# A three-part decoder layer on one core: the first values go to psA, weights' lower halves are made a step later, the last attention step is reordered, and one shared unit moves behind the experts

## The reference

```python
x = x + attn(layernorm(x), Wq, Wk, Wv, Wr)          # 16 heads of 64, causal penalty -50, scale 1/8
x = x + xattn(layernorm(x), ctx, w_q, w_k, w_v, w_o) # the same with keys and values from ctx
x = x + ffn(layernorm(x), ...)
# ffn: shared = swiglu(z @ w_in.T) @ w_out.T         (hidden 512)
#      h = swiglu(z @ w1.T); a gate picks one of 2 groups, then the top 2 of its 4 experts
#      routed = sum over the two of h * weight @ w2[expert].T
```

## Time and profile before

| | us |
|---|---|
| median of 3 runs | 793.65 (792.72 to 795.74) |
| profiled execution | 793.49 |
| its span | 791.7 |
| PE busy in it | 757.6 |
| ACT, DVE, POOL busy | 447.2, 417.9, 281.7 |

### The profile page before, as it was taken

How to read it: one execution, slowest core, us unless ns; L and a number is a source line. 1 busy time by engine, 2 the same in 40 slices (tenths; PEclk the granted TensorE clock), 3 DMA queues, 4 the chain that set the end, 5 groups by cost and what they waited for, 6 DMA issues and landing times. The chain is left out here.

```text
span 791.7 us, 17891 instructions
## 1 busy us (share of the span) xinstructions
PE 757.6 (96%) x6371; PEld 644.6 (81%) x6371; DVE 417.9 (53%) x1265; ACT 447.2 (56%) x1475; POOL 281.7 (36%) x302
## 2 busy tenths in 40 slices
PE   6899999999999999999999999999899998999993
PEld 5688888888888788888888888888667888999883
DVE  6456465456546646543544554465668545333175
ACT  4766556566656767675566566566544435444120
POOL 1553234233422545552243244234102770000475
PEclk9999999999999999999999999999999999999997
DMA  6896000000000202000000002000050555765244
GB/s 197 319 418 225 2 0 0 0 0 0 0 0 2 80 1 81 2 29 1 1 0 26 0 0 104 2 5 24 2 213 26 196 196 184 199 200 174 79 133 140
DMA packets 33608, 64.55 MB, mean 82 GB/s; under 512 B 3412, under 2 KB 15060, under 8 KB 32980
## 3 DMA queue, kind: packets, MB, share of 16 engines
q1 hardware_dynamic: 29172, 51.01, 19.2%
q0 software_dynamic: 4096, 12.59, 4.8%
q10 hardware_dynamic: 288, 0.26, 0.1%
HBM read 38.02 MB, written 30.02 MB: 86 GB/s over the span
## 5 line engine op out<-in xcount | busy, mean ns | idle before, releaser
L445 POOL TENSOR_TENSOR prob<-prob,rsum 128x512 f32<-128x512 f32 x128 | 132.8, 1040 | 332.1 <-DVE rsum L664 332.1
L541 ACT ACTIVATE prob<-psS,nmin 128x128 f32<-128x128 f32 x512 | 182.3, 385 | 21.3 <-DVE nmin L642 15.2
L625 DVE TENSOR_TENSOR oT_lo<-psW,oT_hi 128x512 fp32r<-128x512 f32 x64 | 44.2, 690 | 156.4 <-ACT oT_hi L527 156.3
L541 ACT ACTIVATION_READ_ACCUMULATOR prob<-psS,nmin 128x1 f32 x512 | 115.3, 225 | 0.0
L519 ACT ACTIVATE v<-psW 128x512 f32<-128x512 f32 x64 | 38.2, 597 | 83.4 <-PE psW L144 83.4
L793 PE MATMUL psS<-kt,q 64*128 64x128 f32 x1024 | 74.4, 285 | 0.9 <-DVE kt L617 0.9
L142 PE MATMUL psA<-wo_lo,oT_hi 128*128 128x256 f32 x256 | 73.1, 285 | 0.6 <-DVE oT_lo L625 0.6
L793 PEld LDWEIGHTS psS<-kt,q 64*128 64x128 f32 x1024 | 62.2, 187 | 12.6 <-issue 12.3
L144 PE MATMUL psA<-wo_hi,oT_lo 128*128 128x256 f32 x256 | 72.2, 282 | 0.0
L143 PE MATMUL psA<-wo_hi,oT_hi 128*128 128x256 f32 x256 | 71.8, 281 | 0.0
L1078 POOL DMA_INDIRECT stage<-ys,slot x32 | 35.0, 1092 | 98.9 <-DMA ys<-z 89.4
(11 more groups left out here) (290 smaller groups left out, 1888.5 us busy)
## 6 DMA issues: line engine op xcount, KB each, us to landing
hs<-above SPq DMA_DIRECT2D x1, 9984.0 KB, 30.4
stage<-hs SPq DMA_DIRECT2D x39, 256.0 KB, 3.0
ys<-z SPq DMA_DIRECT2D x39, 128.0 KB, 1.9
w_lo<-w_raw SPq DMA_DIRECT2D x4, 1024.0 KB, 7.8
stage<-ctxT SPq DMA_DIRECT2D x4, 512.0 KB, 4.0
out<-xres SPq DMA_DIRECT2D x16, 128.0 KB
xres<-x SPq DMA_DIRECT2D x3, 512.0 KB, 6.7
stage<-wq SPq DMA_DIRECT2D x2, 512.0 KB, 4.7
```

The costliest lines, as they stand in the source:

```text
L445: nc.gpsimd.tensor_tensor(prob[j % 2][:, r, :], prob[j % 2][:, r, :], rsum[j % 2][:, r].unsqueeze(2).broadcast_to([P, TPG, P]), ALU.mult). ...
L541: e = nc.scalar.activation(prob[j % 2][:, n, :], flat(psS[:])[:, n * P:(n + 1) * P], ACT.Exp, bias=nmin[:, n:n + 1], scale=-1.0, accum_out ...
L625: nc.vector.tensor_tensor(flat(oT[1][:]), psW[:, 1, :], flat(oT[0][:]).bitcast(F32), ALU.subtract).then_inc(oT_lo, 1)
```

## The change

- The value tiles of steps 0 and 1 go into psA: tile 0 ahead of the first scores, tile 1 in step 0, tiles 2 and 3 in step 1. The first z is transposed row tile by row tile as DVE makes it. The lower half of wv is split ahead of the first copies of q and k, and the upper half's lo follows the k copy of step 0.
- DVE copies k ahead of the reciprocals in all steps, and its lower parts of a piece are made there in the step after. wr's lower half changes places with wk's upper half and is split with it in step 1.
- In the last step of attention DVE makes the statistics of the third group behind the copy of pT, and ACT and DVE split the second group's z between the two halves of the exponentials. Biased logits go into above and ties instead of q and kt.
- Behind the last step the weighted values go ahead of the output projection, oT's last parts have a place of their own (`late_oT`, in the context's buffers), and the first block ends with the last output projection. The rest goes to the start of the second block, whose order on PE, ACT and DVE is new: the fourth group's z is transposed into psA ahead of H6, its logits come ahead of H7, their transposes between H7's halves, the counts between H9's halves. ACT makes silu of H7 behind both rounds of exponentials.
- S03 goes behind the experts.

The diff without its unchanged lines (the order of lines left out between two kept ones is that of the kernel):

```diff
@@ -187,6 +187,7 @@
+Z_IN_A = ((1, psA[:, 0, :]), (0, psA[:, 1, :]))
@@ -197,6 +198,14 @@
+def first_z_transposes(pe, halves):
+    for t in range(TPG):
+        pe.wait_ge(z_done, t + 1)
+        for k, bank in halves:
+            mm = nc.tensor.transpose(bank[:, t * P:(t + 1) * P], z[:, t, k * P:(k + 1) * P], ident[:])
+            if t == TPG - 1:
+                mm.then_inc(zT_mm, 1)
@@ -255,8 +264,8 @@
 PIECES = [f"{w} {half}" for w, half in
-          (("wq", "lower"), ("wk", "lower"), ("wv", "lower"), ("wv", "upper"), ("wq", "upper"), ("wr", "lower"),
-           ("wk", "upper"), ("wr", "upper"),
+          (("wq", "lower"), ("wk", "lower"), ("wv", "lower"), ("wv", "upper"), ("wq", "upper"), ("wk", "upper"),
+           ("wr", "lower"), ("wr", "upper"),
@@ -345,6 +354,8 @@
+    late_oT = [c[:, 0, :].rearrange("p (t n) -> p t n", t=TPG) for c in (chi, clo)]
+    FIRST_V = ((1,), (2, 3))
@@ -358,8 +369,8 @@
-               columns(V, wv, upper, 1.0), columns(Q, wq, upper, -SCALE), pair_rows(wr, slice(0, HP)),
-               columns(K, wk, upper, 1.0), pair_rows(wr, slice(HP, PAIRS))]
+               columns(V, wv, upper, 1.0), columns(Q, wq, upper, -SCALE), columns(K, wk, upper, 1.0),
+               pair_rows(wr, slice(0, HP)), pair_rows(wr, slice(HP, PAIRS))]
@@ -369,7 +380,7 @@
-    SWAPS = {(0, 0): ("wq upper", "wr lower"), (0, 1): ("wk upper",), (0, 2): ("wr upper",),
+    SWAPS = {(0, 0): ("wq upper",), (0, 1): ("wk upper", "wr lower"), (0, 2): ("wr upper",),
@@ -385,6 +396,10 @@
+    def oT_of(s):
+        return late_oT if isinstance(s, int) and s == STEPS - 1 else [o[:] for o in oT]
@@ -513,10 +528,10 @@
-        def v_copy(G, half, t, bank):
+        def v_copy(G, half, t, bank, banks=psW):
-            nc.scalar.activation(v[:, t, half * HC:(half + 1) * HC], psW[:, bank, :], ACT.Copy).then_inc(v_copied, 1)
+            nc.scalar.activation(v[:, t, half * HC:(half + 1) * HC], banks[:, bank, :], ACT.Copy).then_inc(v_copied, 1)
@@ -524,7 +539,7 @@
         def oT_split(s):
-            nc.scalar.activation(flat(oT[0][:]), psW[:, 1, :], ACT.Copy).then_inc(oT_hi, 1)
+            nc.scalar.activation(flat(oT_of(s)[0]), psW[:, 1, :], ACT.Copy).then_inc(oT_hi, 1)
@@ -544,20 +559,21 @@
                 elif i == 0:
-                    gate_bias(act, 0, q, 0)
+                    act.wait_ge(slots_zero, 16)
+                    gate_bias(act, 0, above, 0)
+                    z_split_hi(act, L0 + 1, Z_IN_T, z_of[ORDER[1]][0])
             if depth < 2:
-                for t in (2 * j, 2 * j + 1):
-                    v_copy(0, 0, t, (t + 1) % 2)
+                for t in FIRST_V[j]:
+                    v_copy(0, 0, t, t % 2, psA)
-            if after == 2 and j >= ZT_AT:
-                n = j - ZT_AT
-                z_split_hi(act, L0 + n, (Z_MIXED, Z_IN_T)[n], z_of[ORDER[n]][0])
+            if after == 2 and j == ZT_AT:
+                z_split_hi(act, L0, Z_MIXED, z_of[ORDER[0]][0])
@@ -576,8 +592,9 @@
+        first_hi(V)
-        first_hi(V)
+        v_copy(0, 0, 0, 0, psA)
@@ -597,17 +614,15 @@
-        act.preload_act_table(ACT.Silu)
-        gate_bias(act, 1, kt, 0)
+        act.wait_ge(qk_mm, 2 * STEPS)
+        weights_hi(act, N_ATT + 2, wq_hi[:])
+        gate_bias(act, 1, ties, 0)
-        act.wait_ge(qk_mm, 2 * STEPS)
-        weights_hi(act, N_ATT + 2, wq_hi[:])
-        z_split_hi(act, L0 + 2, Z_IN_T, z_of[ORDER[2]][0])
-        gate_bias(act, 2, logitsT, 0)
+        act.preload_act_table(ACT.Silu)
@@ -622,8 +637,11 @@
         def oT_split(s):
-            nc.vector.tensor_tensor(flat(oT[1][:]), psW[:, 1, :], flat(oT[0][:]).bitcast(F32),
-                                    ALU.subtract).then_inc(oT_lo, 1)
+            hi, lo = oT_of(s)
+            nc.vector.tensor_tensor(flat(lo), psW[:, 1, :], flat(hi).bitcast(F32), ALU.subtract).then_inc(oT_lo, 1)
+        def first_lo(n):
+            weights_lo(dve, n, pieces[n][2], pieces[n][1], pieces[n][3])
@@ -650,45 +668,40 @@
             if after == 2:
-                if j == LN_AT:
-                    dve.wait_ge(res_done, NGRP + ORDER[0] + 2)
-                    ln_stats(dve, L0, ORDER[0])
+                n = {LN_AT: 0, LN_AT + 1: 1, PAIRS - 1: 2}.get(j)
+                if n is not None:
+                    dve.wait_ge(res_done, NGRP + ORDER[n] + 2)
+                    ln_stats(dve, L0 + n, ORDER[n])
+            if j + 1 < PAIRS or after < 2:
+                k_copy(G, j + 1)
+            if depth == 0:
+                first_lo(3)
+            for n, by_pool in swaps(G, j - 1):
+                _, hi, lo, scale = pieces[n]
+                if not by_pool:
+                    weights_lo(dve, n, lo, hi, scale)
-                if i == 0 and (j + 1 < PAIRS or after < 2):
-                    k_copy(G, j + 1)
-            if after == 2 and j == LN_AT + 1:
-                dve.wait_ge(res_done, NGRP + ORDER[1] + 2)
-                ln_stats(dve, L0 + 1, ORDER[1])
+                if i == 0 and after == 2 and j == PAIRS - 1:
+                    z_split_lo(dve, L0 + 1, Z_IN_T, z_of[ORDER[1]])
-            if after == 2 and j >= ZT_AT:
-                n = j - ZT_AT
-                z_split_lo(dve, L0 + n, (Z_MIXED, Z_IN_T)[n], z_of[ORDER[n]])
-                ln_rows(dve, L0 + n + 1, ORDER[n + 1])
-                if n == 0:
-                    dve.wait_ge(res_done, NGRP + ORDER[2] + 2)
-                    ln_stats(dve, L0 + 2, ORDER[2])
-            for n, by_pool in swaps(G, j):
-                _, hi, lo, scale = pieces[n]
-                if not by_pool:
-                    weights_lo(dve, n, lo, hi, scale)
+            if after == 2 and j == ZT_AT:
+                z_split_lo(dve, L0, Z_MIXED, z_of[ORDER[0]])
+                ln_rows(dve, L0 + 1, ORDER[1])
-        def first_lo(n):
-            weights_lo(dve, n, pieces[n][2], pieces[n][1], pieces[n][3])
@@ -696,9 +709,8 @@
+        first_lo(V)
-        first_lo(V)
-        first_lo(3)
@@ -721,11 +733,11 @@
+        ln_rows(dve, L0 + 2, ORDER[2])
+        weights_lo(dve, N_ATT + 2, wq_lo[:], wq_hi[:])
-        weights_lo(dve, N_ATT + 2, wq_lo[:], wq_hi[:])
-        z_split_lo(dve, L0 + 2, Z_IN_T, z_of[ORDER[2]])
@@ -761,25 +773,33 @@
-        def v_project(sub, half, t, bank):
+        def v_project(sub, half, t, bank, banks=psW):
             for k in range(KT):
-                mm = product(psW[:, bank, :], (hi[:, k, r], lo[:, k, r]), (wh[V][:, k, c], wl[V][:, k, c]),
+                mm = product(banks[:, bank, :], (hi[:, k, r], lo[:, k, r]), (wh[V][:, k, c], wl[V][:, k, c]),
-        def v_first_half(sub, G, s, tiles=range(TPG)):
+        def v_first_half(sub, G, s):
-            for n, t in enumerate(tiles):
-                if n < 2:
-                    pe.wait_ge((k_copied, q_copied)[n], s + 2)
+            for t in range(TPG):
+                if t < 2:
+                    pe.wait_ge((k_copied, q_copied)[t], s + 2)
+        def very_first_values(tiles):
+            wait_lo(pe, "wv lower")
+            for t in tiles:
+                if t > 1:
+                    pe.wait_ge(v_copied, t - 1)
+                v_project(0, 0, t, t % 2, psA)
@@ -816,10 +836,10 @@
-        def out_project(j):
+        def out_project(j, oT=oT):
             for t in range(TPG):
-                mm = product(psA[:, t // 2, (t % 2) * D:(t % 2 + 1) * D], tuple(o[:, t, :] for o in oT),
+                mm = product(psA[:, t // 2, (t % 2) * D:(t % 2 + 1) * D], (oT[0][:, t, :], oT[1][:, t, :]),
@@ -840,9 +860,7 @@
             if j + 1 < PAIRS or after < 2:
-                if depth == 1:
-                    v_behind = 2
-                elif j == 0 and depth or depth == 2:
+                if j == 0 and depth:
@@ -868,7 +886,7 @@
             if depth < 2:
-                v_first_half(0, 0, s, (2 * j, 2 * j + 1))
+                very_first_values(FIRST_V[j])
@@ -887,8 +905,9 @@
-        z_transposes(pe, 0, Z_FIRST)
+        first_z_transposes(pe, Z_FIRST)
+        very_first_values((0,))
@@ -924,19 +943,10 @@
+        weighted_values(STEPS - 1, PAIRS - 1)
-        weighted_values(STEPS - 1, PAIRS - 1)
-        z_transposes(pe, L0 + 2, Z_IN_T)
-        for k in range(KT):
-            mm = token_half(psS, z_of[ORDER[0]], 0, 1, k)
-        mm.then_inc(ab_mm, 1)
-        out_project(PAIRS - 1)
-        pe.wait_ge(gate_biased, 2)
-        gate_logits(pe, 2, z_of[ORDER[2]], 0)
-        gate_transposes(pe, 0, q)
-        gate_transposes(pe, 1, kt)
-        gate_transposes(pe, 2, logitsT)
+        out_project(PAIRS - 1, late_oT)
@@ -1021,7 +1031,7 @@
-    BEHIND = UNITS.index("S10")
+    BEHIND = UNITS.index("S03")
@@ -1109,17 +1119,19 @@
+        z_split_hi(act, L0 + 2, Z_IN_W, zs[ORDER[2]][0])
-        unit(2)
-        z_split_hi(act, 3 + L0, Z_IN_W, zs[3][0])
+        gate_bias(act, 2, logitsT, 0)
+        z_split_hi(act, L0 + 3, Z_IN_A, zs[3][0])
+        unit(2)
+        act.preload_act_table(ACT.Exp)
+        exps(1)
-        act.preload_act_table(ACT.Exp)
-        exps(1)
@@ -1359,28 +1371,28 @@
```

(54 more changed lines are left out.)

## The result

After: 784.89 us median of 4 runs (784.43 to 785.32); before, beside it, 794.69 (792.72 to 795.96). The ratio is 0.9879, 95% interval 0.9858 to 0.9900: 9.8 us faster, where 11.0 were forecast (782.6). The profiled execution took 785.10 with a span of 783.4, against 793.49 and 791.7. The time lies inside the range; most of what is missing has one place, and I had not seen it.

A forecast was written before the change was run, and what follows sets the result against it. PE, busy 757.6 of 791.7 us, bounds the kernel, with POOL's gathers ending last; gains of 3.7 + 2.75 + 1.75 + 0.5 - 0.5 + 2.8 = 11.0 us give 782.6 us, range 778.8 to 787.2.

The forecast's parts named there:

- Part 1: First three attention steps: first values into psA remove 4.57 us of PE waits, two new waits cost 0.85; gain 3.7 us.
- Part 2: Exchange of weights: pieces' lower halves made a step later, behind the kt copy, remove three PE waits; gain 2.75 us.
- I cost it 0: All attention steps: k's copy ahead of the first reciprocal starts POOL's first product 0.6 to 1.2 us later, covered by slack.
- Part 3: Last attention step: statistics behind the pT copy gain 1.75 us; waits up to the last output projection net 0.5 more.
- Part 4: Start of second block: 2.2 us of waits go, a 2.3 us stall ahead of H9 and 0.35 come; net -0.5 us.
- Part 5: End of kernel: S03 behind the experts lets POOL's gathers start and end earlier; gain 2.8 us.
- the adds bind the end: Rival, end of kernel: DVE's adds stand behind PE's units, so S03 hides nothing; 785.4 us, chance 0.12.
- (a): Rival, second block's start: the gate chain of ACT and DVE slips by one more 2.8 us unit; 785.4 us, chance 0.15.
- (c): Rival, every full step: late reciprocal makes PE wait for prob; at 0.15 us a step 801.4 us, chance 0.03.
- (d): Rival, first steps: the head gives half, as ACT with two weight copies passes the wait on; 784.5 us, chance 0.10.
- (e): Rival, ACT's table load ahead of silu: it drains as the skill page says; 784.0 us, chance 0.05.

The follow-up runs named there:

- e5: Changed kernel with DVE's lower halves of the weights' pieces made at the end of the same step again; 811.16 us.
- e6: Changed kernel with DVE copying k behind the first reciprocal again; 805.79 us, ratio to before 0.9852.
- e0: The changed kernel once more without any edit, as control on a later chip; 805.89 us, ratio to before 0.9895.
- e7: Changed kernel with silu of H7 ahead of the second exponentials, last-step pT copy ahead of the minima, fourth group's shared addition behind S02's last split; 807.45 us, ratio 0.9847.
- e3: Changed kernel with S03 ahead of the experts again; 805.42 us.
- e3b: Changed kernel with S03 ahead of the experts again, repeated on another chip; 807.05 us, ratio to before 0.9876.
- e2: Changed kernel with silu of H7 ahead of the second exponentials and the counts between H10's halves; 803.44 us, ratio to before 0.9855.
- e8: The kernel before, unedited, profiled on a later chip; one run of 811.19 us.
- e1: Changed kernel with ten unread matmul products ahead of H9 to fill PE's stall; 799.41 us.

## Why the prediction was right, and by how much it was off

The mechanisms were right and so was the size up to the stall; one consequence of the stall was missing. That the medians come so near to the forecast (9.8 for 11.0 us) is in part luck: 1.4 of the 9.8 is scatter between executions, and the profiled pair differs by 8.4, which is 2.6 short.

- **Part 1, 3.7 us.** 4.2 came (40.31 to 36.09), 0.16 of it ahead of the first product. The new waits were 0.48 and 0.37, forecast 0.3 and 0.55. The attribution was off: psA is worth 2.84, the other edits of the head 1.2.
- **Part 2, 2.75.** 2.5 came: all three waits went, with 0.28 left at 271.83. e5 shows 3.7 for undoing it, 1.3 of that in the head. "I cost it 0", said of the reciprocals behind k's copy, held in the loops and was wrong at one place: with the lower half there too, POOL's work moved onto the z rows, 0.7 us at 552.
- **Part 3, 2.25.** z's transposes came 8.07 us earlier; less the two parts above that is 1.4, where 1.75 was forecast. They still wait 1.20 us (forecast under 0.3), of which 0.8 is the z rows at 2.09 us (e6, with 1.38, has 0.42). The waits of 0.49 and 0.59 went, and the new one is 0.37 instead of 0.6: 0.7 us for a forecast of 0.5.
- **Part 4, -0.5.** The stall was 2.53, forecast 2.3, by the chain that was counted. From the end of logits 3 (580.40) to H9 the chain takes 8.6 us and PE has 6.1 us of work in it; 8.5 and 6.2 were forecast, though the terms listed there add to 8.3. The table load took 1.28 us and silu followed 1.30 behind its start:

```profile
586.27 1.28 ACT L1120 ACT_TABLE_LOAD   x1
587.57 0.60 ACT L1102 ACTIVATE silu<-psT 128x512 f32<-128x512 f32 x1
```

  **This is the step that failed**: the stall was priced as its own length. It also brings the clock down in most executions, 3.0 us more at H0. The forecast put H0 8.2 us earlier, at 599.9. In e0, where the clock stayed, it starts at 599.14, or 599.76 if its first product came at 10.88 as in after: but for the clock the sum is right to 0.2 us, and the part is -0.4. With the clock it is -3.2 (5.54 less 8.07 less 0.7), outside its bound of -2.0.
- **Part 5, 2.8.** The experts gained 2.5 on H0, because the stall ahead of them grew from 1.41 to 1.82 us: with S03 gone, DVE's addition of the fourth group's shared output, behind S01's product, stands closer to the experts. In e7, which moves it, the stall is 1.41 again, and so it is in e3 and e3b, where S03 is back. The last gather kept 2.55 (8.09 less 5.54). That the adds bind the end was priced at 0.12; it is false on the first chip and true on the three others, for a reason that the prediction doesn't have.
- **The sum.** Up to H0 8.2 were forecast; 5.5 came, and 3.0 went to the clock, so the terms were 0.2 to 0.4 too small. With the 2.5 of part 5 the experts' start is 8.0 earlier, and the profiled pair differs by 8.4 us. The medians differ by 9.8, since before's median beside it was 1.2 above its profiled run and the changed kernel's 0.2 below. The upper bounds of the prediction add to 14.25, not 14.6.
- **Rivals.** (a) No: the chain is 0.2 longer than counted. (c) No: there is no wait for prob in the loops. Its price was wrong: there are 64 steps, not 125, so 0.15 us a step would have been 9.6 us. (d) No, and with part 1 undone only 2.8 come back. (e) No: 1.30 from load to silu.

## What to carry to other kernels

A stall of PE inside an otherwise full stretch has two prices: its length, and what the clock takes behind it; here 2.5 and, in six traces of eight, 1.3 to 4.6 us more. So a reorder that gathers several short waits into one long one can lose what it wins, and the first thing to try is another order of the engine that is late (e2). Work that is moved ahead of a reciprocal on DVE moves POOL's multiplications too, and where these then run beside other rows of DVE it is paid there (0.7 us at 552).

## What the runs showed of the hardware

**The clock falls in a stall or behind it.** In after it was 1.00 during the 2.53 us and fell at 590.2, 1.2 us after PE had work again; in e6 it fell at 587.7, 0.2 us before the stall ended, and in e3 0.4 us before. It came back after 3.4 to 10.2 us, in which PE was busy nearly throughout. At the end of before, PE's last matmuls start at 778.90 and the clock falls with PE idle:

```profile
780.00:782.00 2.00, 0.00 (x0) 1.00 0.67 185
782.00:784.00 2.00, 0.00 (x0) 0.88 0.25 74
784.00:786.00 2.00, 0.00 (x0) 0.50 0.55 157
```

**On three chips the stages with indirect DMAs took up to 20 us more.** On the three later chips ACT idles before silu for a queue that the profile calls remote, although the operands are there (ahead of the first row below, PE's last product for it ended at 610.22). In e0 that idle time is 22.1 us between 600 and 660 and 12.6 between 740 and 780. It includes what ACT has there anyway, 1.2 us a unit in after. Two of the waits read

```profile
611.75 0.60 ACT L1102 ACTIVATE silu<-psT 128x512 f32<-128x512 f32 x1 [2.67 <-remote]
...
763.70 0.60 ACT L1102 ACTIVATE silu<-psT 128x512 f32<-128x512 f32 x1 [12.61 <-remote]
```

In all twelve traces of those chips, before's own (e8) among them, such waits lie only from 600 to 660 and from 740 to 800, the stages in which POOL issues scatters and gathers, and never in attention or between the experts. Ten of the twelve also have such waits of DVE, of 3.7 to 12.4 us, ahead of the additions of shared output. The traces of the first chip have none. It is not a fixed price of a chip either: from H0 to the experts' first transposes it is 65.7 us in e0, 54.5 in e1 and 57.7 in e3 (with S03 in it) on one chip, for 49.2 in after, and the three runs of e1 near 794 us lie 10 or more below its others. What holds ACT there was not found; that the indirect DMAs do is argued from the places only.
